# A two-block Swin transformer on one core: four written-out sequences per group of tiles

## What is computed

```python
def block(x, ...):                      # x: tokens x 192, all in float32
    h = layernorm(x) * g1 + b1
    qkv = windows(roll(h, -4)) @ w_qkv + b_qkv
    a = softmax(q @ k.T * 16 ** -0.5 + bias + mask)     # bias, mask: first block only
    x = x + roll(unwindow(a @ v @ w_proj + b_proj), 4)
    h = layernorm(x) * g2 + b2
    return x + gelu(h @ w_fc1 + b_fc1) @ w_fc2 + b_fc2
```

## Time and profile before

| what | value |
|---|---|
| time, median of 3 runs | 4229.83 us (4226.32 to 4231.19) |
| span of the profiled execution | 4229.7 us |
| TensorE busy | 92% of the span |
| TensorE weight loads busy | 68% |
| VectorE busy | 81% |
| GpSimd busy | 73% |
| ScalarE busy | 64% |
| granted TensorE clock | 0.999 of full |

### The profile page before, as it was taken

One profiled execution on the slowest core, in us unless ns is written; L12 is line 12 of the kernel. 1 busy time (PEld: TensorE's weight loads), 2 busy tenths in 40 slices (PEclk: granted clock), 3 DMA queues, 4 the chain that ended last, 5 costly groups with the idle time before them and its releaser, 6 DMA issues. The chain is left out here.

```text
span 4229.7 us, 174430 instructions
## 1 busy us (share of the span) xinstructions
PE 3910.8 (92%) x65872; PEld 2873.4 (68%) x65872; DVE 3431.5 (81%) x9093; ACT 2718.6 (64%) x5921; POOL 3089.0 (73%) x6257
## 2 busy tenths in 40 slices
PE   3999999999999999999999999999999999999998
PEld 2667667766766776676676677667667766666765
DVE  6888888888888888888888888888888888888885
ACT  1666666666666666666666666666666666666665
POOL 4777777777777777777777777777777777777774
PEclk9999999999999999999999999999999999999999
DMA  4644545545554454555546455455544545554543
GB/s 101 109 92 103 102 98 100 103 101 97 104 101 97 103 103 98 102 100 103 97 102 103 98 100 105 100 99 103 104 94 104 101 98 101 100 105 95 95 98 62
DMA packets 1545149, 421.03 MB, mean 100 GB/s; under 512 B 1441782, under 2 KB 1542522, under 8 KB 1544316
## 3 DMA queue, kind: packets, MB, share of 16 engines
q1 hardware_dynamic: 1540732, 409.87, 49.6%
q10 hardware_dynamic: 3584, 0.01, 0.0%
HBM read 32.15 MB, written 25.17 MB: 14 GB/s over the span
## 5 line engine op out<-in xcount | busy, mean ns | idle before, releaser
L964 DVE TENSOR_TENSOR hid<-scaled,hid 128x512 f16<-128x512 f32 x768 | 677.7, 895 | 348.2 <-POOL hid L1133 328.1
L594 PE MATMUL bank<-w_fc,hid 128*128 128x192 f16 x9216 | 846.1, 246 | 106.1 <-DVE hid L964 104.7
L581 PE MATMUL ps_s<-xh,w_fc 128*128 128x512 f16 x3840 | 866.6, 379 | 70.6 <-ACT stage L705 67.8
L1070 POOL TENSOR_TENSOR rstd<-vare,half 128x2 f32<-128x2 f32 x520 | 361.3, 695 | 766.8 <-DVE vare L904 766.7
L594 PEld LDWEIGHTS bank<-w_fc,hid 128*128 128x128 f16 x9216 | 761.9, 98 | 195.0 <-DVE v_blk L920 169.6
L581 PEld LDWEIGHTS ps_s<-xh,w_fc 128*128 128x128 f16 x3840 | 355.8, 97 | 567.3 <-issue 109.6
L1133 POOL TENSOR_SCALAR hid<-scaled 128x512 f16<-128x512 f32 x768 | 562.9, 738 | 130.6 <-ACT scaled L719 129.2
L719 ACT ACTIVATE scaled<-ps_s,b_fc 128x512 f32<-128x512 f32 x768 | 529.5, 690 | 155.2 <-PE ps_s L581 121.0
L684 ACT ACTIVATE xs<-xn 128x192 f16<-128x192 f32 x512 | 184.8, 361 | 664.3 <-POOL xn L1077 664.3
L711 ACT ACTIVATE pt<-ps_t 128x768 f16<-128x768 f32 x512 | 415.3, 811 | 304.4 <-PE ps_t L538 301.4
L457 PE MATMUL bank<-w_qkv,xh 128*128 128x384 f16 x2560 | 501.8, 326 | 6.2 <-DMA xh<-xs 3.6
(11 more groups left out here) (113 smaller groups left out, 7192.9 us busy)
## 6 DMA issues: line engine op xcount, KB each, us to landing
x_img<-in_x_dram SPq DMA_DIRECT2D x256, 96.0 KB, 2.2
out_dram<-y_img SPq DMA_DIRECT2D x256, 96.0 KB, 2.0
xh<-xs SPq DMA_TRANSPOSE x520, 2.5
qkt<-qk SPq DMA_TRANSPOSE x512, 3.3
ot<-os SPq DMA_TRANSPOSE x512, 2.3
stage<-in_L_conv_fc_w_dram SPq DMA_DIRECT2D x2, 384.0 KB, 4.3
stage<-in_L_conv_w_fc_dram SPq DMA_DIRECT2D x2, 384.0 KB, 4.2
stage<-in_L_conv_qkv_w_dram SPq DMA_DIRECT2D x2, 288.0 KB
```

Source lines behind the costliest of these rows:

```text
L581: last = mm(ps_s[:, u % 2, :].rearrange("p (a t) -> p a t", a=GROUP), w_fc1[layer][:, part, m * 128:(m + 1) * 128], xh[:, p % 2 * GROUP:(p ...
L594: mm(bank[:, 0:C], hid16[:, hs, m, tok], w_fc2[layer][:, ws, m, :], start=(m == 0 and i == 0), stop=False)
L964: v.tensor_tensor(hid16[:, 1, m, :], hid[:, u % 4, :], hid16[:, 0, m, :], ALU.subtract)\
```

## The change

No operation is added, removed or resized. The exceptions by `place` become four separate sequences (place = s % GROUP) on PE, ACT, DVE, POOL and SP, and within them each part has its own visit number. The guards move into the parts. On TensorE the wait for a shared bank is no longer written by hand for each place, but kept by `take`, which remembers the last reader of the bank. The bank that each `mlp_out` uses stays: one in `ps_o`, three in `ps_v`.

```diff
 QK = 3
 AHEAD = 8
-LATE = 8
+FIRST, LAST = -7, TOTAL + 17
...
-                if live(s + 2):
-                    qk_turn(s + 2)
-                if live(s + 5) or live(s + 5 - AHEAD):
-                    norms_turn(s + 5)
-                if live(s - 1):
-                    o_turn(s - 1)
-                if live(s + 9) and s + 9 >= TILES and visit(s + 9)[1] == 0 and visit(s + 9)[0] + 1 < IMAGES:
-                    ge("x_ordered", rank(s + 9) | 1)
-                    load(visit(s + 9)[0] + 1, visit(s + 9)[2])
-                for n, places in ((s - LATE - 2, (0, 1)), (s - LATE - 6, (2, 3))):
-                    if live(n) and visit(n)[1] == 1 and n % GROUP in places:
+                def next_load(n):
+
+                    if live(n) and n >= TILES and visit(n)[1] == 0 and visit(n)[0] + 1 < IMAGES:
+                        ge("x_ordered", rank(n) | 1)
+                        load(visit(n)[0] + 1, visit(n)[2])
+
+                def last_store(n):
+
+                    if live(n) and visit(n)[1] == 1:
                         ge("y_ready", rank(n) | 1)
                         store(visit(n)[0], visit(n)[2])
 
+                place = s % GROUP
+                if place == 0:
+                    norms_turn(s + 4)
+                    next_load(s + 7)
+                    qk_turn(s + 3)
+                elif place == 1:
+                    o_turn(s - 2)
+                    norms_turn(s + 4)
+                    o_turn(s - 1)
+                    norms_turn(s + 5)
+                    next_load(s + 7)
+                    last_store(s - 13)
+                    last_store(s - 12)
+                elif place == 2:
+                    qk_turn(s + 2)
+                    qk_turn(s + 3)
+                    o_turn(s - 1)
+                    next_load(s + 7)
+                    last_store(s - 12)
+                    last_store(s - 11)
+                else:
+                    norms_turn(s + 4)
+                    o_turn(s - 1)
+                    qk_turn(s + 3)
+                    next_load(s + 7)
             run(slot)
             for h in range(2 * SLABS):
...
-                def take_tr(reader, n):
-
-                    ge(*tr_reader)
-                    tr_reader[:] = [reader, n]
+                def take(bank, reader, n):
+
+                    ge(*last_reader[bank])
+                    last_reader[bank] = (reader, n)
...
-                p, place = mlp_phase(s)
-                mlp = 0 <= p < PHASES
-                if mlp and place == 1:
-                    hidden(4)
-                    hidden(5)
-                if live(s + 6) and visit(s + 6)[1] == 0:
+                place = s % GROUP
+                if place == 0:
+                    projection(s - 3)
                     x_transpose(s + 6)
-                if live(s) and place != 1:
+                    y_transpose(s - 10)
+                    shift_scores(s)
+                    pv_product(s - 2)
+                    v_product(s)
+                    hidden((s - 8) // GROUP, 0)
+                    hidden((s - 8) // GROUP, 1)
+                elif place == 1:
+                    hidden((s - 9) // GROUP, 2)
+                    hidden((s - 9) // GROUP, 3)
+                    y_transpose(s - 10)
+                    qk_product(s + 2)
+                    hidden((s - 9) // GROUP, 4)
+                    pv_product(s - 2)
+                    v_product(s)
+                    hidden((s - 9) // GROUP, 5)
+                    projection(s - 3)
+                    p_transpose(s - 1)
                     rel_scores(s)
-                if live(s - 2):
+                    x_transpose(s + 6)
+                    x_transpose(s + 7)
+                    scores(s)
+                    qk_product(s + 3)
+                    mlp_out(s - 9, "v")
+                    shift_scores(s)
+                elif place == 2:
                     pv_product(s - 2)
-                if live(s):
                     v_product(s)
-                if live(s) and place == 1:
+                    projection(s - 3)
+                    y_transpose(s - 10)
                     rel_scores(s)
-                if live(s):
+                    p_transpose(s - 1)
+                    x_transpose(s + 7)
                     scores(s)
-                if live(s - 3):
-                    projection(s - 3)
-                if live(s - 1):
+                    mlp_out(s - 9, "o")
+                    qk_product(s + 3)
+                    shift_scores(s)
+                    mlp_out(s - 8, "v")
+                    rel_scores(s + 1)
+                    projection(s - 2)
+                    pv_product(s - 1)
+                else:
+                    scores(s)
+                    v_product(s)
                     p_transpose(s - 1)
-                if place == 1 and live(s - LATE - 2) and visit(s - LATE - 2)[1] == 1:
-                    y_transpose(s - LATE - 2)
-                if mlp and place == 2:
-                    if visit(p * GROUP)[1] == 1:
-                        y_transpose(p * GROUP)
-                    ge("o_norm", min(s - 2, ENDS))
-                    mlp_out(p * GROUP + 1, ps_o)
-                if mlp and place == 3 and visit(p * GROUP)[1] == 1:
-                    y_transpose(p * GROUP + 2)
-                if live(s):
+                    qk_product(s + 3)
                     shift_scores(s)
-                if live(s + 3):
-                    qk_product(s + 3)
-                if mlp and place == 0:
-                    for m in range(3):
-                        hidden(m)
-                if mlp and place == 2 and visit(p * GROUP)[1] == 1:
-                    y_transpose(p * GROUP + 1)
-                if mlp and place > 0:
-                    ge("v_lo", min(s, ENDS))
-                    if s > ENDS:
-                        ge("resid2", p * GROUP + (0, -1, 0, 2)[place])
-                    mlp_out(p * GROUP + (0, 0, 2, 3)[place], ps_v)
-                if mlp and place == 0:
-                    hidden(3)
-
-            tr_reader = ["x_in", -1]
+                    mlp_out(s - 8, "v")
+                    rel_scores(s + 1)
+                    y_transpose(s - 10)
+                    scores(s + 1)
+                    p_transpose(s)
+
+            mlp_bank = {"v": ps_v, "o": ps_o, "tr": ps_tr, "qk": ps_qk}
+            last_reader = {"tr": ("x_in", -1), "qk": ("qk_lo", -1), "v": ("v_lo", -1), "o": ("o_norm", -1),
+                           "s0": ("exp_done", -1), "s1": ("exp_done", -1)}
...
+                if place == 0:
+                    exp(s - 1)
+                    y_evac(s - 11)
+                    p_hi(s - 1)
+                    exp(s)
+                    load_gelu((s - 8) // GROUP)
+                    gelu((s - 8) // GROUP, 0)
+                    y_evac(s - 10)
+                    x_evac(s + 6)
+                    gelu((s - 8) // GROUP, 1)
+                elif place == 1:
+                    norm2_hi(s - 5)
+                    v_hi(s - 1)
+                    gelu((s - 9) // GROUP, 2)
+                    gelu((s - 9) // GROUP, 3)
+                    qk_hi(s + 2)
+                    y_evac(s - 10)
+                    gelu((s - 9) // GROUP, 4)
+                    v_hi(s)
+                elif place == 2:
+                    gelu((s - 10) // GROUP, 5)
+                    p_hi(s - 2)
+                    x_evac(s + 5)
+                    qk_hi(s + 2)
+                    load_exp((s - 10) // GROUP)
+                    exp(s - 1)
+                    norm2_hi(s - 5)
+                    v_hi(s)
+                    x_evac(s + 6)
+                else:
+                    x_evac(s + 6)
+                    p_hi(s - 2)
+                    y_evac(s - 11)
+                    norm2_hi(s - 5)
+                    qk_hi(s + 2)
+                    exp(s - 1)
...
+                if place == 0:
+                    mlp_residual(s - 9, "v")
+                    p_lo(s - 1)
+                    attention_residual(s - 3)
+                    inverse_sums(s - 2)
+                    o_norm(s - 2)
+                    statistics(s - 3, 1)
+                    mean_variance(s - 3, 1)
+                    statistics(s + 6, 0)
+                    hidden_lo((s - 8) // GROUP, 0)
+                    v_lo(s)
+                    centre(s + 5)
+                elif place == 1:
+                    hidden_lo((s - 9) // GROUP, 1)
+                    hidden_lo((s - 9) // GROUP, 2)
+                    hidden_lo((s - 9) // GROUP, 3)
+                    qk_lo(s + 2)
+                    v_lo(s)
+                    hidden_lo((s - 9) // GROUP, 4)
+                    attention_residual(s - 3)
+                    hidden_lo((s - 9) // GROUP, 5)
+                    p_lo(s - 1)
+                    qk_lo(s + 3)
+                    mlp_residual(s - 9, "v")
+                    mean_variance(s + 5, 0)
+                    statistics(s + 6, 0)
+                    statistics(s - 3, 1)
+                elif place == 2:
```

(69 more changed lines are left out.)

264 lines of the change are left out of this document (131 added, 133 removed).

## The result

The changed kernel takes **4611.1 us** (median of 4 runs, 4600.3 to 4614.2) against 4230.5 us for the kernel before on the same chip: a ratio of **1.0895, with a 95% interval of 1.088 to 1.091**. It is 9% slower. The prediction said 4047 us, with a range of 3945 to 4175, so it had the direction wrong.

A forecast was written before the change was run, and what follows sets the result against it. TensorE, 92% busy, was taken as the bound. Per group 29.56 + 0.24 + 0.45 + 0.38 + 0.1 = 30.73 us against 32.18; the gain of 1.45 times 126 is 183 us, giving 4047 us, range 3945 to 4175.

The forecast's parts named there:

- the three waits: TensorE waiting for `exp` (67.8 us), `hidden_lo` (104.7) and `row_max` (62.3); 1.86 us per group, nearly all expected to go.
- the covers: TensorE work placed over each awaited chain: 1.46 against 1.30 us for `exp`, 2.80 against 2.33 for the last `hidden_lo`.
- the fourth `row_max`: Wait ahead of `shift_scores` for the visit of place 0, its distance staying at 1.4 us; left at 0.1 per group.
- the ceiling by the busy share: Most the change could gain going by TensorE's busy share: 1.86 x 126 = 234 us.
- The new wait: TensorE's `projection` at the start of place 0 waits for `ot` of the place 1 visit: mean 0.45 us per group.
- GpSimd's chain: From `norm2_lo` in place 2 to `o_lo`; with two `order_next`, `ot` lands at 15.5 us against TensorE's 14.76.
- 29.56 of work: TensorE's own work per group in us, summed from start to start, against a measured group of 32.18.
- 0.24 for narrow products: `scores` on TensorE following a full-width product three more times per group, 3 x 0.08 us added.
- small gaps: TensorE products starting a tenth late, 0.76 us per group; half, 0.38, kept in the forecast.
- The 0.76: Small gaps per group in us, by which the trace was said to agree with the skill's page in direction.
- Waits come back on the transposes: Rival: `qk_turn` behind `norms_turn` on SP costs half a microsecond on half the places; group 31.6, 4157 us; chance 0.18.
- Slower: Rival: GpSimd's chain with the `ot` transfer becomes the loop setting the period; at growth 2.0, 4299 us; chance 0.13.

The follow-up runs named there:

- e7: Changed kernel with only its image loads and stores moved to other places of the transposition queue's list: 4369.7 us, ratio 1.032.
- e8: Changed kernel with another transposition queue list: transpositions reordered among themselves, loads and stores moved again, engines' orders unchanged: 4292.8 us, ratio 1.015.
- e9: All five orders rearranged again, starting from the changed engine orders with the list of e8, to leave transpositions slack for late landings: 4141.1 us, ratio 0.979.
- e2: Changed kernel with the transposition queue (SP) list alone put back to the old order: 5682.5 us, ratio 1.343.

## Why the prediction was wrong

*What bounds the kernel, and the three waits.* Right. TensorE has the largest busy share in every run, and the covers were sized well: all three waits went, the fourth `row_max` too (0.9 us left in all, where 0.1 per group was kept). One slip stands beside them: 8% of idle TensorE is 319 us, and the 234 that the text calls the ceiling by the busy share are the three named waits alone.

*The new wait: the step that failed.* The text had one new wait, `projection` on `ot`, at 0.45 us per group, in sum 57 us. It was 141.9, and three more kinds came beside it: 466.6 us, 3.70 per group. The visit of place 1, the one that was meant, has 72.4 of the 141.9, which is close to the 57 by luck. The text had GpSimd finish late and the transposition leave 0.13 us after. In the trace it left 2.3 us after its source was done, in the median of the 82 waits; in e7 1.2, and in e8, with the same order on GpSimd and another list, 0.13, and there the wait is 3.6 us. So GpSimd's chain had the slack that the sum denied it, and the queue did not have the readiness that the sum took for granted. Three things were missing from that step.

First, **the queue**. The transpositions were costed from the end of their producer: "0.13 to reach SP and 2.3 to land". The list on SyncE was read for the transpositions' order only. The loads and stores, 0.5 us of issue each and at times a wait of their own, stand in the changed list directly ahead of a `norms_turn`, `o_turn` or `qk_turn` that has no slack any more, and were priced at nothing. Moving them away gives 241 of the 381 us back (e7); a list that also changes the order of the transpositions among themselves another 77 (e8, which moves loads and stores once more, so the 77 are not split).

Second, **the landing time was a median**. The earlier trace rows give 3.3 and 2.3 us, and one transposition in four or five takes about 1.5 us more. Both kernels have these; the one before never noticed, because each transposition had a step of slack (its waits for them are 7 us in all). "No `ot` transfer was ever urgent before, so its 2.3 was never tested" was the right doubt, put in the rival at 0.13, and put there for one chain alone.

Third, **the products behind a wait**. The sum had no term for them, and they are 152 us, 1.2 per group: and 86 of them are in `hidden`. The granted clock over the run is 0.97 of the full 2.4 GHz, and 3% of 4612 us is 138 us, which is most of the 152; in e9, which hardly waits, it is 0.998, in e2, which waits most, 0.86. The rows show it one wait at a time: 2.75 us idle, then 20 chunks' products in 6.16 us instead of 4.49; 2.02 and 0.37 us idle, then a `qk_product` of 1.78, about the lower level of 1.2 GHz. A wait of 2.12 us was not followed by slow products. Over the run after its first 200 us, the trace shows the lower level beginning within 1.5 us of the end of 48 of TensorE's 59 idle stretches of 2 to 3 us, and of 16 of its 252 of 0.5 to 2 us. So the wait of 2.75 us cost 1.67 more in what followed it, and such a thing happens behind most of the long waits and few of the short ones.

*The sum.* 29.56 of work, 0.24 for narrow products, 3.70 of transfer waits and 1.21 of slower products make 34.7 against the measured 35.40. What is left, 0.7, is the "small gaps" of which 0.38 were kept. In e9 the group is 376.3 us over 12, or 31.36, with only 0.55 of named waits, so 30.8 is what TensorE needs with full clock; 29.56 + 0.24 + 0.76 is 30.6. So **the small gaps look like work, not gaps**: they did not go where the waits went. The forecast's 30.73 lies just below that: it would have asked for no waiting at all. The Trainium skill (Perfetto Trace Analysis, Identifying the Most-Contended Engine) takes the weight loads' busy share, beside the share of peak arithmetic, and not the matmuls' busy share, as the measure of how close TensorE is to its limit. Here e9 stands at 70% by the weight loads and 96% by the matmuls, and with named waits of 70 us in all it is the matmuls' share that told how little a new order could still gain. The 0.76 in which the prediction saw the trace agree with the page was no room.

*The rivals.* The result is outside all of them. "Waits come back on the transposes" had the mechanism: `qk_turn` and `norms_turn` behind one another, and its two marks came true (the new entry for `xh` over 60, that for `qkt` over 60). It was priced at 0.9 us per group over the forecast, a fifth of what came. "Those queue places have about 1 us of slack" fell by the 1.5 of a late landing alone. "Slower" had the direction and the wrong loop: with GpSimd's order unchanged and only the list new (e8), the wait at the end of that chain fell from 72.4 to 3.6 us and 318 of the 381 us came back.

*The marks.* `load_gelu` 35.40 apart, not 30.7; the three old waits below 10, 10 and 40 as said; the new entry for `ot` at 142, under the 150 at which the text would have named GpSimd's chain, and rightly not named; VectorE at 72%, not 84 to 86, since the group got longer and its own busy time fell from 3431 to 3308 us.

## What to carry to other kernels

When a change makes the engines' orders tight, the in-order queue that carries the data between them has to be laid out as strictly as they are: write down each issue in it, loads and stores too, and ask of each what stands behind it and when that is needed. Cost a transfer that becomes urgent at its late landings, not at the median, and look for those in the trace of before, where they are there and harmless. And count a long wait of TensorE at more than its length, since what follows it may run at the lower clock.

## What the runs showed of the hardware

A DMA transposition with an instruction-fetch packet in the middle of its flight lands late: with the computation left out, 2.7 us became 3.4 to 4.2 for 46 of 47 transpositions beside 6000 small products, which draw a packet every 3.8 us, and 2 of 120 were late beside 1700 large ones, which drew 13 packets in 369 us; of the 296 without a packet in flight none was late. In the changed kernel it was 317 of 578 with a packet and 2 of 710 without. What in the fetch holds the transposition's packets up is open. So is what decides whether TensorE's clock falls behind a wait, and why TensorE's busy time in e9 is 71 us longer than before at a full clock.
